# Ten layer normalisations with centring products and moved loads, and a local attention that sorts its sums on GpSimd, in a four-block transformer kernel

## The reference

```python
x = x + _L0_attn_ref(_layernorm(x), ...)   # block A: 2 layers, full attention (2 heads) and FFN
x = x + _L0_ffn_ref(_layernorm(x), ...)    # block F: 2 layers, windowed attention (8 heads) and GEGLU FFN
x = x + _L1_attn_ref(_layernorm(x), ...)   # block G: local attention (16 heads of 8) and latent attention
x = x + _L1_ffn_ref(_layernorm(x), ...)    # block M: mixture of 64 experts

m = x.mean(-1, keepdims=True)              # a layer's own normalisation, twice in a layer of A, once in one of F
v = ((x - m) ** 2).mean(-1, keepdims=True)
(x - m) / jnp.sqrt(v + 1e-05) * g + b
```

## Time and profile before

| | us |
|---|---|
| median of three runs (lowest, highest) | 1461.59 (1457.17, 1467.51) |
| the profiled execution, its span | 1462.01, 1460.2 |
| busy PE, DVE, ACT, POOL | 1174.1, 948.0, 595.1, 387.2 |
| n0 to n6, all ten (rows 1 shows seven; the second n2 14.8, the second n4 21.2, n5 23.6) | 186.1 |
| local attention | 98.6 |
| the three stages A1 (behind n1), A4 (behind n2), F4 (behind n4) | 20.9, 33, 34 |

### The profile page before, as it was taken

How to read it: one execution, slowest core, us unless ns; L and a number is a source line. 1 busy time by engine, 2 the same in 40 slices (tenths; PEclk the granted TensorE clock), 3 DMA queues, 4 the chain that set the end, 5 groups by cost and what they waited for, 6 DMA issues and landing times. The chain is left out here.

```text
span 1460.2 us, 28689 instructions
## 1 busy us (share of the span) xinstructions
PE 1174.1 (80%) x11181; PEld 722.2 (49%) x11181; DVE 948.0 (65%) x1629; ACT 595.1 (41%) x1370; POOL 387.2 (27%) x294
## 2 busy tenths in 40 slices
PE   7699887899787769887767889656995789973897
PEld 5477644577534337653336753523653254432243
DVE  3577543777456867434885723487698469988577
ACT  2455343655334649433557822300552245520100
POOL 0256400566103865200884500333000000000000
PEclk9899998899998989979997989889897799985699
DMA  1000001000012210011220010000000011110001
GB/s 53 19 1 1 2 1 42 1 1 2 1 51 59 52 33 3 2 60 22 54 52 2 3 60 3 20 3 4 4 4 13 0 24 22 18 37 1 8 29 43
DMA packets 52905, 29.41 MB, mean 20 GB/s; under 512 B 35522, under 2 KB 46252, under 8 KB 52268
## 3 DMA queue, kind: packets, MB, share of 16 engines
q1 hardware_dynamic: 52780, 27.65, 7.8%
HBM read 18.44 MB, written 1.06 MB: 13 GB/s over the span
## 5 line engine op out<-in xcount | busy, mean ns | idle before, releaser
L252 POOL TENSOR_TENSOR A_pr<-A_pr,A_rs 128x1024 f32<-128x1024 f32 x64 | 121.1, 1893 | 79.6 <-DVE A_rs L315 77.2
L305 DVE TENSOR_REDUCE A_mx<-psb 128x1 f32<-128x1024 f32 x64 | 77.8, 1216 | 15.9 <-PE psb L265 15.8
L985 POOL TENSOR_TENSOR F_raw<-F_raw,F_rc 128x1024 f32<-128x1024 f32 x32 | 75.4, 2356 | 38.6 <-DVE F_raw L1060 38.6
L348 ACT ACTIVATE A_pr<-psb,A_nm 128x1024 f32<-128x1024 f32 x64 | 71.2, 1113 | 20.1 <-DVE A_nm L309 20.1
L1004 PE MATMUL psb<-F_wqkv,F_hst 128*128 128x512 f32 x128 | 65.6, 637 | 16.5 <-ACT F_hst L1076 16.5
L286 PE MATMUL psb<-A_pt,A_V 128*64 128x128 f32 x1024 | 63.0, 275 | 13.8 <-issue 8.9
L1015 PE MATMUL psb<-ident,F_raw 128*128 128x128 f32 x256 | 38.6, 299 | 42.1 <-POOL F_raw L988 42.0
L275 PE MATMUL psb<-ident,A_pr 128*128 128x128 f32 x512 | 69.4, 279 | 1.4 <-ACT A_pt L355 1.4
L1674 ACT ACTIVATE M_hall<-psb,M_bu 128x512 f32<-128x512 f32 x64 | 44.0, 687 | 64.6 <-PE psb L1625 64.5
L1867 PE MATMUL psb<-M_hb,M_wd 128*128 128x512 f32 x128 | 70.1, 630 | 0.0
L286 PEld LDWEIGHTS psb<-A_pt,A_V 128*64 128x64 f32 x1024 | 56.2, 137 | 25.9 <-issue 21.7
(11 more groups left out here) (331 smaller groups left out, 2961.3 us busy)
## 6 DMA issues: line engine op xcount, KB each, us to landing
F_VS<-F_V SPq DMA_DIRECT2D x62, 128.0 KB, 2.3
F_raw<-in_c_xpos_dram SPq DMA_DIRECT2D x3, 1024.0 KB, 4.9
F_wqkv<-in_L_ffn_wqkv_dram SPq DMA_DIRECT2D x3, 768.0 KB, 6.2
A_rot<-in_c_rot_dram SPq DMA_DIRECT2D x2, 512.0 KB
A_w<-in_L_attn_w_dram SPq DMA_DIRECT2D x4, 256.0 KB
M_wu<-in_L_ffn_Wup_dram SPq DMA_DIRECT2D x16, 64.0 KB, 2.0
M_wg<-in_L_ffn_Wgate_dram SPq DMA_DIRECT2D x16, 64.0 KB, 2.1
M_wd<-in_L_ffn_Wdown_dram SPq DMA_DIRECT2D x16, 64.0 KB, 1.7
```

The source lines that it names most:

```text
L252: pool.tensor_tensor(p, p, rs[:, u % 2:u % 2 + 1].broadcast_to([P, SEQ]), ALU.mult).then_inc(scaled, 1)
L305: dve.tensor_reduce(mx[:, u % 2:u % 2 + 1], sview(u), AX, ALU.max).then_inc(maxed, 1)
L348: act.activation(pr[:, u % NP, :], sview(u), ACT.Exp, bias=nm[:, u % 2:u % 2 + 1], scale=scale, accum_out=su[:, u % 2:u % 2 + 1]).then_inc ...
L985: pool.tensor_tensor(rs[:, o, :], rs[:, o, :], rc[:, o, :], ALU.add).then_inc(unit, 1)
```

## The change

- `layer_norm`: PE multiplies by `centre` (identity minus 1/128), so that `bank[c]` holds the deviations at once. ACT squares them out of PSUM, DVE copies them to `n_xc` (`hold`, with the gain in it). The averages go to two banks, root and reciprocal run on each half of the tokens, and the spread products go to two further banks. PE's order interleaves the three kinds. A square root of one column (`warm`) stands first on ACT.
- With the shift (n4) no copy is made: two products for each chunk, of the tokens and of the tokens one earlier, with `centres[0]` and `centres[1]`, each half of the matrix.
- Loads: block A's 13 attention weights of layer 0 and `rot` are issued in n0, its 5 FFN weights in A1, the next layer's 13 attention weights in A4. Block F's next attention weights move from n4 to F4. n3, n5 and n6 keep theirs.
- `local_attention`: DVE adds both rows' sums in one instruction into `acc` (two for a tile). POOL sorts them: a product with `halves`, an addition, twice for a tile. DVE's swap, bias, inverse and product (`norm`) follow one tile later. `NP` (buffers of exponentials) goes from 3 to 2.
- At the start DVE builds the three matrices.

```diff
-                    dve.memset(ones_mean[:], 1.0 / P)
+                    dve.memset(mean[:], 1.0 / P)
+                    for i in range(2):
+                        r = slice(64 - 64 * i, 128 - 64 * i)
+                        dve.memset(centres[i][r, :], 0.0)
                     dve.memset(eps[:], EPS).then_inc(made, 1)
                     dve.wait_ge(loaded, 32)
+                    for i in range(2):
+                        r = slice(64 * i, 64 * i + 64)
+                        dve.tensor_scalar(centres[i][r, :], ident[r, :], 1.0 / P, None, ALU.subtract)
+                    dve.tensor_scalar(centre[:], ident[:], 1.0 / P, None, ALU.subtract)
...
+
+                    @block.tensor
+                    def _(pe):
+                        def deviate(c):
+                            if add is not None:
+                                pe.wait_ge(moved, c + 1)
...
+                                o = 1 if c * CH % SEQ == 0 else 0
+                                pe.matmul(bank[c], centres[0][:], src[:, cs(c)], start=True, stop=False)
+                                last = pe.matmul(psb[:, c, o:CH], centres[1][:], src[:, c * CH + o - 1:(c + 1) * CH - 1], start=False, stop=True)
                             else:
-                                dve.scalar_tensor_tensor(out=dst[:, cs(c)], in0=xc[:, cs(c)], scalar=gain, in1=bank[c],
-                                                         op0=ALU.mult, op1=ALU.mult).then_inc(scaled, 1)
+                                last = pe.matmul(bank[c], centre[:], src[:, cs(c)], start=True, stop=True)
+                            last.then_inc(centred, 1)
+
+                        def average(c):
+                            pe.wait_ge(squared, c + 1)
+                            for t in range(4 * c, 4 * c + 4):
+                                last = pe.matmul(psb[:, 4 + c // 2, t % 8:t % 8 + 1], sq[:, t * P:(t + 1) * P], mean[:], start=True, stop=True)
+                            last.then_inc(var_rdy, 1)
+
+                        def distribute(c):
+                            pe.wait_ge(inv, c // 2 + 1)
+                            if c >= 2:
+                                pe.wait_ge(scaled, c - 1)
+                            for j in range(4):
+                                t = 4 * c + j
+                                last = pe.matmul(psb[:, 6 + c % 2, j * P:(j + 1) * P], rstd[:, t:t + 1].broadcast_to([P, P]), ident[:], start=True, stop=True)
+                            last.then_inc(spread, 1)
+
+                        deviate(0)
+                        deviate(1)
+                        average(0)
+                        deviate(2)
+                        average(1)
+                        deviate(3)
+                        average(2)
+                        distribute(0)
+                        average(3)
+                        for c in range(1, NCH):
+                            distribute(c)
...
+                        act.activation(warm[:], eps[:, 0:1], ACT.Sqrt)
+
+                        def square(c):
                             act.wait_ge(centred, c + 1)
-                            act.activation(sq[:, cs(c)], xc[:, cs(c)], ACT.Square).then_inc(squared, 1)
-                        act.wait_ge(var_rdy, 1)
-                        act.activation(rstd[:], psb[:, 4, 0:NT], ACT.Sqrt, bias=eps[:, 0:1]).then_inc(std_rdy, 1)
+                            act.activation(sq[:, cs(c)], bank[c], ACT.Square).then_inc(squared, 1)
+
+                        def root(h):
+                            act.wait_ge(var_rdy, 2 * h + 2)
+                            act.activation(rstd[:, 8 * h:8 * h + 8], psb[:, 4 + h, 0:8], ACT.Sqrt, bias=eps[:, 0:1]).then_inc(std_rdy, 1)
+                        square(0)
+                        square(1)
+                        square(2)
+                        root(0)
+                        square(3)
+                        root(1)
...
+                    @block.vector
+                    def _(dve):
+                        def invert(h):
+                            dve.wait_ge(std_rdy, h + 1)
+                            dve.reciprocal(rstd[:, 8 * h:8 * h + 8], rstd[:, 8 * h:8 * h + 8]).then_inc(inv, 1)
+
+                        def hold(c):
+                            dve.wait_ge(squared, c + 1)
+                            if gain is None:
+                                dve.tensor_copy(xc[:, cs(c)], bank[c]).then_inc(held, 1)
+                            else:
+                                dve.tensor_scalar(xc[:, cs(c)], bank[c], gain, None, ALU.mult).then_inc(held, 1)
+
+                        def scale(c):
+                            dve.wait_ge(spread, c + 1)
+                            dve.wait_ge(held, c + 1)
+                            dve.tensor_tensor(dst[:, cs(c)], xc[:, cs(c)], psb[:, 6 + c % 2, :], ALU.mult).then_inc(scaled, 1)
+                        if add is not None:
+                            for c in range(NCH):
+                                dve.tensor_tensor(src[:, cs(c)], src[:, cs(c)], add[:, cs(c)], ALU.add).then_inc(moved, 1)
+                        hold(0)
+                        hold(1)
+                        hold(2)
+                        invert(0)
+                        hold(3)
+                        scale(0)
+                        invert(1)
+                        for c in range(1, NCH):
+                            scale(c)
...
-                "local", "scored exped mixed cleared added swapped biased inverted normed")
+            NP = 2
...
-                        pool.memset(own, 0.0)
-                        pool.memset(total, 0.0).then_inc(cleared, 1)
+                        pool.memset(acc, 0.0).then_inc(cleared, 1)
+                        for n in range(NT):
+                            m = mine[:, n % 2, :, :]
+                            j = both[:, n % 2, :, :]
+                            x = acc[:, :, n * P:(n + 1) * P]
+                            pool.wait_ge(added, 2 * n + 2)
+                            for i in range(2):
+                                if n or i:
+                                    pool.wait_ge(joined, 2 * n + i)
+                                pool.tensor_tensor(m, x, halves[:, 2 * i:2 * i + 2].unsqueeze(2).broadcast_to([P, 2, P]), ALU.mult).then_inc(parted, 1)
+                                pool.wait_ge(parted, 2 * n + i + 1)
+                                if n >= 2:
+                                    pool.wait_ge(normed, n - 1)
+                                pool.tensor_tensor(j[:, i, :], m[:, 0, :], m[:, 1, :], ALU.add).then_inc(joined, 1)
...
-                                pe.wait_ge(added, 8 * (n - 1))
+                                pe.wait_ge(added, 2 * (n - 1))
...
+                        def add(n):
+                            dve.wait_ge(mixed, 2 * n + 2)
+                            for c in range(2):
+                                w = BROAD if (n + 1) % TPS else P - 64 * c
+                                x = acc[:, :, n * P + 64 * c:n * P + 64 * c + w]
+                                if c:
+                                    dve.wait_ge(added, 2 * n + 1)
+                                dve.tensor_tensor(x, x, vview(n, c)[:, :, 0:w], ALU.add).then_inc(added, 1)
+
+                        def norm(n):
+                            own, total = (both[:, n % 2, i, :] for i in range(2))
+                            dve.wait_ge(joined, 2 * n + 2)
+                            if n:
+                                dve.wait_ge(normed, n)
+                            dve.stream_shuffle(sums[:], total, [(i + 16) % 32 for i in range(32)]).then_inc(swapped, 1)
+                            dve.wait_ge(swapped, n + 1)
+                            dve.scalar_tensor_tensor(out=own, in0=sums[:], scalar=bias, in1=own, op0=ALU.mult, op1=ALU.add).then_inc(biased, 1)
+                            dve.wait_ge(biased, n + 1)
+                            dve.reciprocal(sums[:], sums[:]).then_inc(inverted, 1)
+                            dve.wait_ge(inverted, n + 1)
+                            dve.tensor_tensor(result[:, n * P:(n + 1) * P], own, sums[:], ALU.mult).then_inc(normed, 1)
...
+                            if n:
+                                dve.wait_ge(added, 2 * n)
+                            add(n)
+                            if n:
+                                norm(n - 1)
+                        norm(NT - 1)
...
+            layer_norm("n0", X, H, loads=lambda sp, sem: issue(sp, sem, attention_weights(0) + [(rot[:], a["c_rot"])]))
...
+                layer_norm("n1", H, XL, g1[:, 0:1], b1n[:, 0:1])
...
+                        @block.sync
+                        def _(sp, l=l):
+                            sp.wait_ge(loaded, issue(sp, loaded, ffn_weights(l)))
...
+                    @block.sync
+                    def _(sp, l=l):
+                        sp.wait_ge(loaded, issue(sp, loaded, attention_weights((l + 1) % LAYERS)))
...
```

(5 more changed lines are left out.)

145 lines of the change are left out of this document (42 added, 103 removed).

## The result

The changed kernel takes 1419.9 us (median of four runs, 1409.8 to 1428.2), the kernel before 1461.1 over four runs: a ratio of 0.973, 95% interval 0.969 to 0.977. The forecast was 1423 us, in a range of 1408 to 1443. The profiled execution took 1428.2 us (span 1426.4) and is the slowest of the four; the granted clock of the four is 0.906, 0.912, 0.913 and 0.918, from the slowest to the fastest.

What follows compares the result with a forecast made beforehand. No engine bounds the whole: PE bounds n2, loads the first n1, SP n5, VectorE local attention. 1462.0 - 27.7 - 10.5 = 1423.8 us, or 1423 against the median; range 1408 to 1443.

Steps and rivals of the forecast that it cites:

- -27.7 in the norms: Ten normalisations: new form, moved loads and clock allowances together save 27.7 us.
- -10.5 in local attention: Local attention: PE replaces VectorE as the bound at 4.80 us a tile; the stage saves 10.5 us, to 88.
- The clock term: Normalisations: a stage loses 0.9 us to a lowered clock; 2.2 in n0, 2.3 in second n1, 1.7 in n3.
- rival 2: Normalisations: clock stays full inside a stage, six allowances of 0.9 us fall away, total 1418 us; chance 0.12.
- Rival 4: Normalisations: mixed product order keeps PE at 1.2 GHz throughout, +63 us there, total 1514 us; chance 0.04.
- n1's loads: First n1: 6.3 us of the stage before the change are waiting for loads.
- n5: n5: SP's 53 loads stay and end the stage, so it saves 0 and remains at 23.6 us.
- Rival 3: Local attention: GpSimd becomes the bound and the stage is as before, total 1434 us; chance 0.06.
- The moved loads at nothing: A1, A4 and F4: the loads moved there cost nothing, since no engine waits for SP before the stage's end.
- all else at nothing: Stages outside the normalisations and local attention: they keep their work and their time, a change of 0 us.

Runs made afterwards that it cites:

- experiment 4: Changed kernel with PE's four centring products ahead of the averages in all normalisations: 1425.2 us, ratio 0.975.
- experiments 5 and 6: Changed kernel: n3's PE waits for all adds, 1425.3 us; that plus n3's centring products first, 1418.2; instead four unread products after first block's gated unit, 1425.4.
- experiment 3: Changed kernel with the first block's loads back in n1, 1439.5 us; changed kernel with the old normalisation form and loads still moved, 1437.9 us.

## Why the prediction was right, and where it was not

- *The sum.* Forecast -27.7 in the norms and -10.5 in local attention. In the first profile the norms' own lengths give -27.6 (158.5 against 186.1) and local attention -11.3. That the first agrees within a tenth is luck: n3 was 6.4 us over its forecast and most others 0.9 under theirs.
- *The clock term was the wrong size.* I allowed 0.9 us in each stage; in n1, n2, n4, n6 nothing was lost, and these stages have the lengths worked out for 2.4 GHz: 12.86 for 12.9, 15.98 for 15.9, 12.10 for 12.1. In these stages rival 2 had it right. The order of products is the cause in the first n1, n2 and n6 [experiment 4]; the first n4 keeps 1.00 in the dense order too. n0 lost 1.5 us for 2.2 forecast (nothing in four of the later profiles), the second n1 came at 18.35 for 18.2, and n3 at 14.3 for 14.2 where it was not caught (14.65 to the next stage).
- *Rival 4's mechanism exists*, in single stages. I had set against it that centring products are dense; in n3 they stood two at a time and in the caught profile did not bring the clock back. It costs 6 to 8 us in one stage, not 63. What decides whether a stage is caught stays open [experiments 5 and 6].
- *n1's loads* were priced right in the first n1: 6.5 us by experiment 3, 6.3 in the prediction. For n4's I had nothing, and 2.9 of n4's 5.3 us went when they did, with a higher clock; no run shows whether by them.
- *n5*: unchanged for 23.6 forecast, 23.2 measured, ended by SP.
- *Local attention*: 87.3 for 88. VectorE by the groups has 3.22 us a tile (3.2 forecast), GpSimd's four instructions 2.15 (2.6 with waits forecast). The bias takes 570 ns in the mean beside GpSimd, and 352 in the kernel before, with the sorting on VectorE, and in the last tile, where GpSimd has finished. The Trainium skill (SBUF — State Buffer, "Who interferes with whom") states that a VectorE instruction with two inputs in SBUF contends with a GpSimd instruction that reads SBUF; these rows agree. The last product of a tile also has two such inputs, and I had counted it in: it stays at 292 ns for 291. The 0.2 us cost nothing where PE bounds the tile. Rival 3 is out.
- *The moved loads at nothing*: right within 0.4 us, as far as A1 (20.9 to 21.3), A4 and F4 at clock 1.00 show. The second A4 stands at 0.95 and 34.5 us with the new norms and its loads, at 1.00 and 32.9 in the kernel before, and at 1.00 and 32.9 with the old norms and its loads: again the clock, and not the loads alone.
- *The total*: 1419.9 and 1415.9 for 1423. That it came so near is in part luck. I had all else at nothing, and against the profile before it is 5 us more in the first profile and 11 us less in the second, mostly in stages whose code is unchanged and whose clock differs; 1428 and 1406 us were profiles of the same program.

## What to carry to other kernels

Look for what ends a stage before making its work faster: n1 and n5 hung on SP's queue, and moving loads gave 14 us, nearly as much as the new form, and 10 us more where the change had not looked. A restructured step can move the first use of a loaded value forward; with the loads left in place it then costs more than the old one. For the clock, try mixing kinds of products where PE is hardly idle before the stage: in n2 and n6 it was worth 1 to 3 us a stage. And read length, count and clock of a stage together, in more than one profile: one execution shows one of several outcomes.

## What the runs showed of the hardware

- The granted clock fell with PE never idle behind 24 passes of single-column averages (n2 in dense order: PE busy from 173.52, at half from 179.41), and in the kernel before behind 32 of them and 0.65 us of idle time. It stayed at 1.00 with the same passes in eights between centring products, in all eleven profiles with that order (n2, both times).
- With that order the clock can also stay at 0.50 for 17.1 us of uninterrupted products (n3, 20.65 us long) and for 20.5 us with 19.6 of PE in them (second n1, 25.97 us).
- The same program spreads over 21 us from run to run, and two of its profiles differ by 22.2 us, of which 21.8 lie in six places: n3, the expert block, the two stages ahead of n6, A1 and the first A4.
- On VectorE a sum of 384 elements with PSUM takes 554 ns, one of 192 with a mask 418; a reciprocal of 128 columns 953.
